# A two-layer transformer block: a router and its scatters run inside the last attention steps, and a reordered start of the feed-forward

## The reference, cut to what matters

```python
x = x + gate0 * spectral_mixer(layernorm(x))                     # layer 0
h = layernorm(x) * (1 + scale1) + shift1
g = gelu_tanh(h @ w1 * s1) * (h @ w2 * s2)                        # gated, 128 -> 512
x = x + gate1 * (gelu(gelu(g @ h1) @ h2) @ w3)                    # 512 -> 512 -> 512 -> 128
h = layernorm(x) * (1 + scale2) + shift2                         # layer 1
o = softmax(q(h) k(h)^T / sqrt(8)) v(h)                          # 16 heads, no mask
x = x + gate2 * (o @ fc + bias)
h = layernorm(x) * (1 + scale3) + shift3
logits = relu(h @ rw1) @ rw2                                     # the router, 128 -> 512 -> 8
top2, weights = top_k(logits, 2), softmax over the two
x = x + gate3 * sum(weights[e] * (relu(h @ W1[e]) @ W2[e]) for e in top2)
```

## Time and profile before

| what | us |
|---|---|
| median of three runs (1125.94 to 1132.19) | 1128.51 |
| the profiled execution: device time | 1128.35 |
| its span, first to last instruction | 1126.5 |
| busy PE, DVE, ACT, POOL | 1033.0, 829.9, 799.4, 172.5 |

### The profile page before, as it was taken

The page is one execution under the profiler, slowest core; times in us unless marked ns, Lnnn a source line. Parts: engine busy times, 40 slices in busy tenths (PEclk is TensorE's granted clock), DMA queues, the critical chain, the costliest instruction groups (busy, mean ns, idle before and its releaser), DMA issues.

```text
span 1126.5 us, 21109 instructions
## 1 busy us (share of the span) xinstructions
PE 1033.0 (92%) x8426; PEld 559.5 (50%) x8426; DVE 829.9 (74%) x1170; ACT 799.4 (71%) x1542; POOL 172.5 (15%) x217
## 2 busy tenths in 40 slices
PE   3878889989999999999999999999999998869995
PEld 3645668763433333333333333333333447748984
DVE  4768433368879999999999999999999306144544
ACT  2655543447579999999999999999999784107664
POOL 1002000016470000000000000000000102543552
PEclk9899999999989999999999999999999998659997
DMA  7000000000000101100110111011000000135653
GB/s 288 1 1 0 1 1 0 1 1 1 1 1 2 30 3 31 31 24 9 31 31 13 20 31 31 2 30 31 2 1 2 2 2 3 40 100 172 201 171 121
DMA packets 35952, 41.19 MB, mean 37 GB/s; under 512 B 2924, under 2 KB 27119, under 8 KB 35472
## 3 DMA queue, kind: packets, MB, share of 16 engines
q1 hardware_dynamic: 33072, 32.83, 10.6%
q0 software_dynamic: 2496, 4.27, 1.1%
q10 hardware_dynamic: 288, 2.76, 0.6%
HBM read 25.36 MB, written 15.15 MB: 36 GB/s over the span
## 4 chain that ended last, share of the span: by engine, by line
DVE 49%; PE 40%; issue 4%; ACT 4%; DMA 2%; another core or an unknown queue 1%; POOL 0%; POOLq 0%; SPq 0%; DVEq 0%; ACTq 0%
DVE mx L1662 42%; PE ps L982 5%; PE ps L983 4%; PE ps L984 4%; PE ps L1171 4%; PE ps L1109 4%; PE ps L1354 3%; PE ps L1056 3%; PE ps L1078 2%; PE ps L963 2%; PE ps L1019 1%; PE ps L1256 1%; DMA x<-x_in 1%; PE ps L910 1%
## 5 line engine op out<-in xcount | busy, mean ns | idle before, releaser
L1662 DVE TENSOR_REDUCE mx<-ps 128x2 f32<-128x1024 f32 x512 | 586.3, 1214 | 18.9 <-PE ps L1078 18.8
L761 ACT ACTIVATE probs<-ps 128x512 f32<-128x512 f32 x1024 | 540.9, 598 | 54.1 <-PE ps L1171 46.2
L1171 PE MATMUL ps<-Qb,Ks 32*128 32x512 f32 x1024 | 329.9, 496 | 0.5 <-ACT probs L761 0.5
L1109 PE MATMUL ps<-probs,V 128*16 128x256 f32 x4096 | 320.8, 386 | 7.0 <-ACT U L755 7.0
L1078 PE MATMUL ps<-Ks,Qb 32*128 32x512 f32 x1024 | 255.3, 497 | 1.0 <-DVE mx L1662 0.7
L1171 PEld LDWEIGHTS ps<-Qb,Ks 32*128 32x128 f32 x1024 | 149.4, 182 | 215.0 <-issue 123.3
L1109 PEld LDWEIGHTS ps<-probs,V 128*16 128x16 f32 x4096 | 67.2, 94 | 134.4 <-issue 77.5
L1078 PEld LDWEIGHTS ps<-Ks,Qb 32*128 32x128 f32 x1024 | 95.0, 182 | 34.2 <-DVE mx L1662 18.3
L496 POOL TENSOR_SCALAR mhi<-mn 128x16 fp32r<-128x16 f32 x16 | 4.2, 261 | 422.3 <-DVE mn L1670 422.3
L829 ACT ACTIVATE eh<-ps,b 128x256 f32<-128x256 f32 x92 | 36.7, 477 | 28.4 <-PE ps L984 26.7
L568 POOL DMA_INDIRECT yk<-ye,target x46 | 47.3, 1028 | 57.0 <-DVE ye L1894 45.0
(11 more groups left out here) (302 smaller groups left out, 1313.2 us busy)
## 6 DMA issues: line engine op xcount, KB each, us to landing
w<-moe_in SPq DMA_DIRECT2D x23, 512.0 KB
buf<-zeros SPq DMA_DIRECT2D x11, 792.0 KB, 6.3
gz<-buf SPq DMA_DIRECT2D x23, 132.0 KB
FW<-ffn_in SPq DMA_DIRECT2D x1, 2824.5 KB, 12.4
yin<-yk SPq DMA_DIRECT2D x4, 512.0 KB
SW<-spectral_in ACTq DMA_DIRECT2D x1, 1479.5 KB, 9.3
DW<-mods_in ACTq DMA_DIRECT2D x1, 1219.0 KB, 5.7
x<-x_in SPq DMA_DIRECT2D x4, 256.0 KB, 10.7
```

The source lines that it names most:

```text
L761: act.activation(probs[:, 4 * ((s + 2) % 4) + g, :], score(n), ACT.Exp, scale=SCALE1) \
L1109: last = pe.matmul(ps[32 * g:32 * g + VW, 6, queries], V[:, kt, col:col + VW], probs[:, 4 * ((s + 2) % 4) + g, queries], start=(kt == 0 an ...
L1171: pe.matmul(score(n), Ks[rows, hg, kt * P:kt * P + P], Qb[rows, hg, :], start=True, stop=True).then_inc(sem.st_ready, 1)
L1662: dve.tensor_reduce(mx[:, k // 16 % 2, k % 16 // 4, k % 4, 2 * pair:2 * pair + 2], ps[:, at:at + 2, :], AX, ALU.max).then_inc(sem.bank_rea ...
```

## The change

In short:

- `ahead(n)` follows a table `tail` of 40 entries. Beside `heads` and `fc` it holds, for blocks 0 to 2, `turn_z`, `router` (one of its four 128-row parts at a time, three matmuls), `router_scores` (a quarter at a time, four matmuls) and, for blocks 0 and 1, `places`. `keep_warm` is gone; six entries are empty. The last quarter of block 2's scores, `places(2)` and all of block 3 stay behind attention.
- For these three blocks DVE does what ACT and POOL did: the inverse square root with a first guess from the number's bits and three Newton steps (`root_inverse`, 12 small instructions), the modulation, the second parts and the relus. Block 3 keeps ACT's square root, modulation and relu; its second part moves to DVE.
- POOL splits the router's first weight earlier (after group 13) and can scatter block b as soon as its slots are there.
- The front of the feed-forward: the norm of layer 0's second half is cut in two pieces (block 0, and blocks 1 to 3) rather than four; the second parts of `act_a` for blocks 0 and 1 go to POOL, the first part of `h2` to ACT, its second part to POOL in four pieces; PE turns blocks 1 to 3 within or behind `ffn_hidden(0, 0)`; ACT copies the gains and modulates blocks 1 to 3 between gelus.
- The query stack of block 0 is projected before the key stack of block 3, and that before the wait for block 3's norm.
- Steps 0 and 1 of attention have four pairs of unread matmuls in place of the value matmuls, and the zeroing of bank 6 stands in step 2 of DVE rather than ahead of step 0.
- Eight unread matmuls ahead of the first expert tile become three.

```diff
+        tail = (("heads", 0), ("fc", 0), ("heads", 1), None, ("fc", 1), ("heads", 2), None, ("fc", 2), ("turn_z", 0), None,
...
-        stacks = [(0, 0, tb) for tb in range(TB)] + [(1, 0, 0)] + [(0, 1, tb) for tb in range(TB)] \
+        stacks = [(0, 0, tb) for tb in range(TB - 1)] + [(1, 0, 0), (0, 0, TB - 1)] + [(0, 1, tb) for tb in range(TB)] \
...
-        norms = [(k, a, b) for k, parts in enumerate((((0, 16),), ((0, 4), (4, 8), (8, 12), (12, 16)), ((0, 12), (12, 16)), ((0, 12), (12, 16)))) for a, b in parts]
+        norms = [(k, a, b) for k, parts in enumerate((((0, 16),), ((0, 4), (4, 16)), ((0, 12), (12, 16)), ((0, 4), (4, 8), (8, 12), (12, 16)))) for a, b in parts]
...
# POOL
-            pool.tensor_copy(h2_[0][:, :], fw["h2"]).then_inc(sem.weight_split, 1)
+            for n in range(FB):
+                second_part(n)
             pool.wait_ge(sem.weight_split, 1)
-            pool.tensor_tensor(h2_[1][:, :], fw["h2"], h2_[0][:, :].bitcast(F32), ALU.subtract) \
+            for fb in range(FB):
+                part_h = slice(fb * FF, fb * FF + FF)
+                pool.tensor_tensor(h2_[1][:, part_h], fw["h2"][:, part_h], h2_[0][:, part_h].bitcast(F32), ALU.subtract) \
...
+            for n in range(FB, 2 * FB):
+                second_part(n)
# ACT
             ffn_gates(0)
...
-            ffn_b(0)
-            ln_std(1, 8)
-            ln_std(1, 12)
-            ffn_gates(1)
-            ffn_c(0)
-            ln_out(1, 2)
-            ln_out(1, 3)
+            ln_std(1, 4)
+            ffn_b(0, (gains, lambda: ln_out(1, 1), split_h2))
+            ffn_gates(1, lambda: ln_out(1, 2))
+            ffn_c(0, lambda: ln_out(1, 3))
# PE
-            pe.wait_ge(sem.hT_ready, 2)
-            ffn_hidden(0, 0)
-            pe.wait_ge(sem.hT_second, 2)
-            ffn_up(1)
-            pe.wait_ge(sem.weight_split, 2)
-            ffn_hidden(0, 1)
+            ffn_hidden(0, 0, lambda: z_transposes(1, 1))
             pe.wait_ge(sem.bcast_copied, 2)
             z_transposes(1, 2)
             z_transposes(1, 3)
+            pe.wait_ge(sem.hT_second, 2)
+            ffn_up(1)
+            pe.wait_ge(sem.weight_split, 5)
+            ffn_hidden(0, 1)
...
-            keep_busy(2).then_inc(sem.busy_done, 1)
-            pe.wait_ge(sem.busy_done, 1)
-            pe.wait_ge(sem.u_zero, 1)
+            keep_busy(2)
...
-            unread(1, 8)
+            unread(1, 3)
# DVE
+            def root_inverse(b):
+                mine, at = cols(b, 4), 11 * b
+                y = rstd[:, mine]
+                dve.wait_ge(sem.stats, 32 * 3 + 8 * (b + 1))
+                dve.tensor_scalar(root[:, 0, :], mv[:, mine, 1], 1e-5, None, ALU.add).then_inc(sem.root_step, 1)
+                dve.tensor_scalar(root[:, 1, :], mv[:, mine, 1], 1e-5, -0.5, ALU.add, ALU.mult).then_inc(sem.root_step, 1)
+                dve.wait_ge(sem.root_step, at + 2)
+                dve.tensor_scalar(y.bitcast(I32), root[:, 0, :].bitcast(I32), -0.5, 1597463007.0, ALU.mult, ALU.add) \
+                   .then_inc(sem.root_step, 1)
+                for n in range(3):
+                    dve.wait_ge(sem.root_step, at + 3 + 3 * n)
+                    dve.tensor_tensor(root[:, 2, :], y, y, ALU.mult).then_inc(sem.root_step, 1)
...
+            def relu(tb, fb):
...
+                dve.tensor_scalar(rh[:, tb % 2, fb, :], bank(rh_bank(tb, fb)), mw["rb1"][:, fb:fb + 1], 0.0, ALU.add, ALU.max) \
+                   .then_inc(sem.rh_copied, 1)
```

More of the change, by code:

```diff
@@ L185, in adaln_pair @@
         rank = sb("rank", [P, 4, EXP], side="right")
+        root = sb("root", [P, 3, 4], side="right")
         chosen = sb("chosen", [P, NT, 2, EXP], side="right")
@@ L972, in z_transposes @@
                 last.then_inc(sem.zT_ready, 1)
-            for b in range(2):
-                z_transposes(1, b)
+            z_transposes(1, 0)
             pe.wait_ge(sem.x1_ready, TB)
@@ L1113, in values, with first_steps @@
                     last.then_inc(sem.pv_ready, 1)
+            def first_steps():
+                for _ in range(2):
+                    last = pe.matmul(bank(6), Ks[:, 0, 0:P], Ks[:, 0, 0:512], start=True, stop=True)
+                return last
             def keep_busy(count):
@@ L1119, in keep_busy @@
                 return last
-            def keep_warm():
-                for g in (2, 3):
-                    rows = slice(32 * g, 32 * g + 32)
-                    pe.matmul(bank(g), Ks[rows, 0, 0:P], Ks[rows, 0, 0:512], start=True, stop=True)
             def heads(b):
@@ new lines, in router, with router_scores @@
+            def router(tb, fb):
+                pe.wait_ge(sem.weight_split, 7)
+                pe.wait_ge(sem.hT_second, TB + tb + 1)
+                if 1 < 4 * tb + fb < 12:
+                    pe.wait_ge(sem.rh_copied, 4 * tb + fb - 1)
+                three(bank(rh_bank(tb, fb)), both(rw1_, every, slice(fb * P, fb * P + P)), both(hT1, every, cols(tb, 512)),
+                      True, True).then_inc(sem.rh_ready, 1)
+            def router_scores(tb, qt):
+                if qt == 0:
+                    pe.wait_ge(sem.rh_copied, 4 * tb + 4)
+                    pe.wait_ge(sem.aux_ready, max(3, tb + 1))
+                    if tb in (1, 2):
+                        pe.wait_ge(sem.prod_made, tb)
+                for fb in range(FB):
+                    last = pe.matmul(ps[:, last_turn, qt * EXP:qt * EXP + EXP], rh[:, tb % 2, fb, qt * P:qt * P + P],
+                                     mw["rw2"][:, fb * EXP:fb * EXP + EXP], start=(fb == 0), stop=(fb == FB - 1))
+                if qt == 3:
+                    last.then_inc(sem.sc_ready, 1)
@@ new lines, in places @@
+            def places(tb):
+                pe.wait_ge(sem.moe_consts, 1)
+                pe.wait_ge(sem.index_real, 1)
+                pe.wait_ge(sem.sc_read, tb + 1)
+                pe.wait_ge(sem.picked, tb + 1)
+                to = ps[:, place_bank(tb), 0:4 * EXP].rearrange("p (q e) -> p q e", e=EXP)
+                pe.matmul(to, cw["ones"][0:1, :], wide(index_f[0:1, base_at:base_at + EXP], [1, 4, EXP], 1),
+                          start=True, stop=False, skip_group_check=True)
+                for q in range(3):
+                    pe.matmul(to[:, q + 1:4, :], cw["ones"], wide(picks[:, 4 * tb + q, :], [P, 3 - q, EXP], 1),
+                              start=False, stop=False, skip_group_check=True)
+                for b in range(tb):
+                    pe.matmul(to, cw["ones"], wide(part[:, b, :], [P, 4, EXP], 1), start=False, stop=False, skip_group_check=True)
+                pe.matmul(to, lower[:, :], picks[:, 4 * tb:4 * tb + 4, :], start=False, stop=True,
+                          skip_group_check=True).then_inc(sem.place_ready, 1)
@@ new lines, in ahead @@
+            def ahead(n):
+                if tail[n] is None:
+                    return
+                stage, b = tail[n][0:2]
+                if stage == "heads":
+                    heads(b)
+                elif stage == "fc":
+                    fc(b)
+                elif stage == "turn_z":
+                    turn_z(b)
+                elif stage == "router":
+                    router(b, tail[n][2])
+                elif stage == "scores":
+                    router_scores(b, tail[n][2])
+                else:
+                    places(b)
@@ L1281, in _ @@
+            pe.wait_ge(sem.hT_ready, TB * 2 + 3)
             heads(3)
[L1282 removed]
             fc(3)
[L1284 to L1287 removed]
             turn_z(3)
[L1289 to L1295 removed]
             places(2)
[L1297 removed]
+            for fb in range(FB):
+                router(3, fb)
@@ L1298, in _ @@
+            for qt in range(4):
+                router_scores(3, qt)
             places(3)
+            pe.wait_ge(sem.prod_made, 3)
             for b in range(TB):
-                last = pe.matmul(ps[:, 0, 0:EXP], cw["ones"], part[:, b, :], start=(b == 0), stop=(b == TB - 1))
+                last = pe.matmul(ps[:, 2, 0:EXP], cw["ones"], part[:, b, :], start=(b == 0), stop=(b == TB - 1))
             last.then_inc(sem.count_ready, 1)
```

347 lines of the change are left out of this document (186 added, 161 removed).

## The result

| what | before | after |
|---|---|---|
| median, us | 1127.4 (4 runs) | 1154.9 (4 runs) |
| ratio to before, with its 95% interval | | 1.0253 [1.0199, 1.0307] |
| profiled execution / span | 1128.35 / 1126.5 | 1154.6 / 1152.4 |
| start to step 236 (first `heads`) | 876.0 | 860.4 |
| from there to the end of the value matmuls (the tail) | 54.0 | 125.6 |

I forecast 1114, with 1103 to 1127 as the range. The differences of the four stretches are -15.6, +71.6, -30.0 and -0.1, together +25.9, which is the difference of the spans. Three of them came out near the forecast (-13.8, -31.8, 0); the tail did not (+31.4).

What follows compares the result with a forecast made beforehand. PE was taken as busy in the last 20 steps with DVE free, and one block's chain of small steps as deciding behind attention. 31.4 - 31.8 - 10.8 - 3 = -14.2 from 1128.35 gave 1114 us, range 1103 to 1127.

Steps and rivals of the forecast that it cites:

- Term 1: Last 20 attention steps: moved work lengthens PE's half steps, 50.9 to 82.3 us, +31.4, if PE never waits for DVE.
- The slower rival: Last 20 steps: PE waits for late DVE relus and picks and drops to half clock; 1142 us, chance 0.08.
- Term 2: Path behind attention to the first expert matmul gets shorter: -31.8 us, between -37 and -26.
- The rival of the hold that comes back: PE's signals are held back 8.85 us again as POOL scatters: 1123, or 1132 with two holds; chance 0.15.
- Term 3: Feed-forward front: PE's waits and a half-clock stretch go, -10.8 us, between -5 and -14.
- The held-up DVE parts: Front: POOL's subtractions might hold up DVE's norm and `act_b` parts by up to 1.3 each; two make it 2.6 worse.
- Term 4: Two small edits, a stack ahead of the last norm and attention's start: -1.5 us each, -3 together.

Runs made afterwards that it cites:

- e8: Kernel before with only the change's front, stacks and attention start, plus score matmuls behind attention widened from 8 to 128 columns: 0.982 times the kernel before.
- e7: Kernel before with only the change's front, stacks and attention start; block 1's scatters wait for block 2's scores to be read: 1099.7 us, ratio 0.986.
- e13: Kernel before with only the change's front, stacks and attention start; none of the 32 scatters goes before block 3's slots are ready: 1132.5 us.
- e10: Changed kernel with the scores' 8 columns repeated to 128 and the 24 and 32 of `places` to 96 and 128: 1124.4 us, ratio 0.999.
- e2: Kernel before with unread matmuls of the changed kernel's shapes, 8-column ones included, in `keep_warm`'s places in the last 20 steps: 1199.3 us.
- e4: Changed kernel with one unread 448-column matmul ahead of each of the 11 score quarters in the last 20 steps: 1158.4 us, ratio 1.030.
- e14: Same edit as e7 (block 1's scatters behind block 2's scores), on a chip where the hold may show: 1114.8 us, ratio 0.988.
- e16: Kernel before with the change's front, stacks and attention start, scores repeated to 128 columns, block 1's scatters behind block 2's scores: 1102.3 us, ratio 0.977.
- e12: Kernel before with only the change's front, stacks and attention start, scores and `places` behind attention repeated to 128 columns: ratio 0.987.
- e11: Kernel before with only the change's front, stacks and attention start, a repeat run on another chip: 1109.8 us, ratio 0.983.

## Why the prediction was wrong

**Term 1, the last 20 steps (+31).** This is the step that failed. Its working at full clock stands: I put a half step with a router part at 2.1 and one with scores at 2.33, and they took 2.31 and 2.39. By the rows at full clock the 22 half steps from 896.4 on (9 scores, 8 router parts, 2 places at 2.56, a turn at 1.99, 2 empty at 0.98) and the last value matmuls would take 51.4 us; they took 89.5. So of the +71.6, 38.1 are the half clock and 33.5 the term that I forecast as 31.4. The condition that I set, "if PE never waits there for DVE", was met, and it was not enough. I took the price of a quarter from the scores behind attention, and for the clock asked only whether PE would be idle. Those same scores had the answer: in the kernel before the clock falls at 944.8, at the end of block 0's, at 955.0, 0.1 behind block 1's (951.14 + 3.72), and at 961.9, amid block 2's, which takes 5.91 us for it. The prediction counts with half clock behind attention and with a quarter at full clock in the tail, and never asks what brought the clock down there; e8 beside e7 shows that these falls go with the 8 columns.

**The slower rival** named 1142 and had the right consequence (half clock, a router part at twice its price) with the wrong cause, PE waiting for relus and picks. PE was busy in every microsecond of it. The stand-in run with no reader at all fell all the same.

**Term 2, the path behind attention (-32).** Right: -30.0. Value matmuls to block 3's slots took 36.1 where I had counted 33.3; 2.9 of it is a hold, which I had left out. The rival of the hold that comes back was right as a mechanism, at a third of its size, and the run without scatters (e13) has none. POOL's scatters within attention did no harm in the changed kernel; in e10, at full clock, a DVE relu came late just behind a row of them.

**Term 3, the front (-11).** Right: the loop starts 12.7 us earlier. The held-up DVE parts did not come: DVE's `act_b` subtraction at 116.45 took 0.72 amid POOL's four of 115.34 to 120.81. By the rule of the Trainium skill (SBUF — State Buffer, Who interferes with whom), as I applied it, DVE would have been held up and the sum 2.6 worse. The trace shows a hold-up the other way round: POOL's second subtraction, begun under DVE's, took 1.75 where the other three took 1.28 to 1.30, and nothing waited for it.

```profile
116.58 1.75 POOL L508 TENSOR_TENSOR h<-FW,h 128x512 fp32r<-128x512 f32 x1
```

**Term 4 (-3).** Right in sum: 14.8 earlier at the score pair at 244.59, of which 2.1 are new, and 15.6 at step 236: 2.9 where 3 was forecast.

**The sum** was -14.2. With the measured stretches and the tail at full clock it would have been -15.6 + 33.5 - 30.0 - 0.1 = -12.2, still inside my range. Even so the change would have been worth less than its front: the run with the columns repeated (e10) loses 14.6 against the front alone, where I had weighed +31.4 against -31.8 and called it even.

## To carry to other kernels

Before matmuls are moved into a stretch that runs at full clock, look at their columns, not only at whether the engine stays busy: a few matmuls of 8 to 32 columns brought PE to half clock amid unbroken work, and what stood behind them took 1.8 times as long (a half step with scores 4.24 rather than 2.39 us). Where an operand is that narrow, reading it several times by a stride of zero costs next to nothing (1.16 against 1.06 us for four), and in e10 it kept the clock until PE had to wait. And a change in several parts is best timed in parts: here one part, the front, carried the whole gain, and the largest part lost it again.

## What was not expected of the hardware

- Four matmuls of 8 columns last 1.06 us at full clock, four of 128 columns 1.16; the weight loads take 0.97 us in both.
- The granted clock fell with PE busy 36.40 of 36.40 us. The Trainium skill (TensorE: Matmul & The Clock Gate, HAM oscillation — how this bites in real kernels) tells of the fall behind waits for transfers; by that rule the tail should have stayed at 2.4 GHz, and the measurement decides against it for matmuls this narrow. The fall in e10 does come behind a wait, though one of 2.3 us for DVE and not for a transfer.
- Once down, the clock stayed at 0.5 for 88.7 us, through eight router parts of 512 columns as well. With the scores widened it came back once after 10.2 us, amid quarters of 128 columns, and the second time only after 30.7 us. There, and in the changed kernel (both times), e2, e4 and e10, it came back within the last row of value matmuls, which has no score matmuls between. Why it came back there and not on the router parts is open.
- What PE signals to DVE and ACT can arrive late while POOL sends a row of 8 or 16 indirect scatters: by 11.3 us in e14, by nothing in e13, which has no scatters in that stretch. Most held waits end within 2.4 us of the end of such a row; three end in the middle of one (e16 at 960.50, e2 at 1048.37, e12 at 983.43). In the four profiles of one chip, and in e11, there is none, so the scatters alone don't decide it.
